# Sixteen heads of 8 on one core: the stack's ones by DMA, its zeros on VectorE, the first loads among the weights

## The reference

```python
x = x + L0_xattn(layernorm(x), ctx);  x = x + L0_ffn(layernorm(x))   # a0, f0
x = x + L1_xattn(layernorm(x), ctx);  x = x + L1_ffn(layernorm(x))   # a1, f1
x = x + L2_xattn(layernorm(x), ctx);  x = x + L2_ffn(layernorm(x))   # own, cross, f2
x = x + L3_xattn(layernorm(x), ctx);  x = x + L3_ffn(layernorm(x))   # a3, f3
```

```python
qh = heads(q @ Wq + bq);  kh = heads(k @ Wk + bk);  vh = heads(v @ Wv + bv)   # H = 16, D = 8
attn = softmax(einsum('bhqd,bhkd->bhqk', qh, kh) / sqrt(8), axis=-1)
out = concat(einsum('bhqk,bhkd->bhqd', attn, vh)) @ Wo + bo
```

## Time and profile before

| | |
|---|---|
| median of three runs | 8348.56 us |
| the profiled execution, its own time | 8347.76 us |
| its span | 8346.0 us |
| mean granted TensorE clock | 0.924 of full speed |
| busy: PE, VectorE, ACT, POOL | 7304.8, 5939.8, 4935.5, 2515.7 us |
| load blocks of a0, a1, a3 begin | 6.27, 1848.45, 6711.54 us |

### The profile page before, as it was taken

One profiled execution on the slowest core, in us unless ns is written; L12 is line 12 of the kernel. 1 busy time (PEld: TensorE's weight loads), 2 busy tenths in 40 slices (PEclk: granted clock), 3 DMA queues, 4 the chain that ended last, 5 costly groups with the idle time before them and its releaser, 6 DMA issues. The chain is left out here.

```text
span 8346.0 us, 186132 instructions
## 1 busy us (share of the span) xinstructions
PE 7304.8 (88%) x73814; PEld 3269.2 (39%) x73814; DVE 5939.8 (71%) x12851; ACT 4935.5 (59%) x9814; POOL 2515.7 (30%) x2443
## 2 busy tenths in 40 slices
PE   5999999877999997677679999999998759999979
PEld 2333333352333333344424444444444523333335
DVE  3888888646888896666646666666665438888855
ACT  3777777635888884333345555555554228888852
POOL 4222222123211210343334445445444232212200
PEclk9999999987999998677879999999999769999989
DMA  3334433204334420000100000000000133334310
GB/s 84 79 91 95 90 79 79 52 17 94 83 78 95 94 64 28 15 14 13 41 16 9 8 7 8 7 8 7 5 4 18 47 69 88 82 85 95 85 29 13
DMA packets 318099, 412.61 MB, mean 49 GB/s; under 512 B 56341, under 2 KB 237861, under 8 KB 317240
## 3 DMA queue, kind: packets, MB, share of 16 engines
q1 hardware_dynamic: 315704, 400.18, 20.7%
q10 hardware_dynamic: 1536, 0.53, 0.0%
HBM read 225.41 MB, written 174.66 MB: 48 GB/s over the span
## 5 line engine op out<-in xcount | busy, mean ns | idle before, releaser
L669 ACT ACTIVATE a_probs<-scores_ps 128x512 f32<-128x512 f32 (+2 forms) x5248 | 2819.4, 589 | 495.9 <-PE scores_ps L587 401.7
L728 DVE TENSOR_REDUCE a_unit_max<-bank 128x1 f32<-128x512 f32 x3072 | 2002.6, 682 | 197.0 <-PE bank L574 185.7
L604 PE MATMUL bank<-a_probs,a_v_sb 128*9 128x256 f32 (+1 forms) x20992 | 1619.4, 380 | 51.3 <-ACT a_out_sb L676 51.2
L587 PE MATMUL scores_ps<-a_stack 64*128 64x256 bf16 (+1 forms) x10496 | 1379.4, 274 | 13.5 <-ACT a_probs L669 9.5
L1268 ACT ACTIVATE cross_probs<-scores_ps 128x512 f32<-128x512 f32 (+1 forms) x1792 | 869.4, 570 | 777.9 <-PE scores_ps L1165 777.9
L1348 DVE TENSOR_REDUCE cross_unit_max<-bank 128x1 f32<-128x512 f32 x1536 | 1005.3, 686 | 326.0 <-PE bank L1151 322.4
L574 PE MATMUL bank<-a_stack 63*128 63x512 bf16 (+2 forms) x3413 | 1199.6, 375 | 6.4 <-DMA a_stack<-a_stack_dram 2.2
L1435 POOL TENSOR_TENSOR cross_added<-cross_probs 128x1024 f32<-128x1024 f32 x384 | 902.9, 2351 | 949.3 <-PE bank L1198 860.3
L728 DVE TENSOR_REDUCE a_unit_max<-scores_ps 128x1 f32<-128x512 f32 x1536 | 1047.8, 682 | 180.6 <-PE scores_ps L574 175.5
L797 POOL CAST a_parts<-a_qk 128x512 bf16<-128x512 f32 (+3 forms) x240 | 125.9, 525 | 1933.2 <-ACT a_qk L688 1841.1
L574 PE MATMUL scores_ps<-a_stack 63*128 63x512 bf16 (+2 forms) x1707 | 640.2, 375 | 36.2 <-DMA a_stack<-a_stack_dram 33.6
(11 more groups left out here) (417 smaller groups left out, 10423.7 us busy)
## 6 DMA issues: line engine op xcount, KB each, us to landing
a_stack_dram<-a_parts SPq DMA_DIRECT2D x288, 400.2 KB, 4.3
a_stack<-a_stack_dram SPq DMA_DIRECT2D x256, 348.2 KB, 7.9
a_stack<-a_stack_dram SPq DMA_DIRECT2D x128, 444.2 KB, 9.6
a_ctxT<-in_ctxT SPq DMA_DIRECT2D x48, 400.2 KB, 4.9
a_stack_dram<-a_parts SPq DMA_DIRECT2D x288, 64.0 KB, 2.6
a_stack_dram<-a_parts SPq DMA_DIRECT2D x96, 128.0 KB, 2.6
f_x<-x_after_dram SPq DMA_DIRECT2D x32, 256.0 KB, 3.2
x_after_dram<-a_res SPq DMA_DIRECT2D x48, 128.0 KB, 4.9
```

Source lines behind the costliest of these rows:

```text
L587: ins = pe.matmul(score_bank[(2 * e.i + a) % 3][0:n, j * TOK + q0:(j + 1) * TOK], stack[p][rows(a, 64), 2 * e.g + j, k0:k0 + n], stack[p][ ...
L604: ins = pe.matmul(out_bank[32 * h:32 * h + V8, q0:TOK], v[0:n, e.t, 4 * e.g + h, :], A.probs[0:n, held, o + q0:o + TOK], start=(e.t == 0), ...
L669: act.activation(by_pair(A.probs[0:n, b, a * 512:(a + 1) * 512])[:, :, q0:TOK], by_pair(score_bank[(2 * e.i + a) % 3][0:n, :])[:, :, q0:TO ...
L728: ins = dve.tensor_reduce(unit_max[:, e.g % 2, qt, 2 * a + j, c:c + 1], bank[:, 0:e.s.chunks[c][1]], AX.X, ALU.max)
```

## The change

- `prepare` no longer fills the stacks. It sets one tile `ones_k` of 16 partitions by KW columns to one (KW is 1857 or 1601), and in the values only the ninth column of each head.
- The zeros of both stacks are set by VectorE at the end of the bias block.
- The ones of rows 48 to 63 and 112 to 127 are copied from `ones_k` by four DMAs at the head of SP's part of the main block; each writes 16 partitions by 8 by KW. TensorE waits for them ahead of its first unit.
- ctxT and x of batch 0 are loaded in the load block, behind the weights.
- The five splits of the lead-in are made by VectorE and no longer by POOL; those of later batches stay on POOL.

```diff
@@ prepare
-            for s in stack:
-                chain(pool.memset(s[:, :, KW:W], 0.0))
-                for a in range(2):
-                    chain(pool.memset(s[64 * a + 32:64 * a + 64, :, 0:KW], 1.0))
+            chain(pool.memset(ones_k[:, :], 1.0))
             for vs in v_sb:
                 for v in vs:
-                    chain(pool.memset(v[:, :, :, :], 1.0))
+                    chain(pool.memset(v[:, :, :, 8:9], 1.0))
             L.prepare(pool, chain)
 
-        load_weights(nc, ctx, stage, [(W_sb[n][...], w[n]) for n in names_w + names_b], prepare)
+        load_weights(nc, ctx, stage, [(W_sb[n][...], w[n]) for n in names_w + names_b] + [
+            (ctxT[0][:, :], G.ctxT[0]), (x_sb[0][:, :, :], x_in[0].rearrange("(t p) c -> p t c", p=P))], prepare)
@@ bias block, VectorE
                 dve.memset(out_bank[:, :], 0.0)
+                for held in stack:
+                    dve.memset(held[:, :, KW:W], 0.0)
@@ new function
+        def split(eng, e):
+            made = e.cur + 1
+            c, k = piece(e.j), n_pieces * made + e.j + 1
+            eng.wait_ge(S["side_done"], e.after)
+            if e.j == 0 and made >= 1:
+                eng.wait_ge(S["parts_out"], 16 * outs * made)
+            eng.tensor_copy(parts[:, 0, c], qk[:, c]).then_inc(S["part0"], 1)
+            eng.wait_ge(S["part0"], k)
+            eng.tensor_tensor(qk[:, c], qk[:, c], parts[:, 0, c], ALU.subtract).then_inc(S["left"], 1)
+            eng.wait_ge(S["left"], k)
+            eng.tensor_copy(parts[:, 1, c], qk[:, c]).then_inc(S["part1"], 1)
+            eng.wait_ge(S["part1"], k)
+            eng.tensor_tensor(parts[:, 2, c], qk[:, c], parts[:, 1, c], ALU.subtract).then_inc(S["part2"], 1)
@@ program_sync
-            sp.dma_start(ctxT[0][:, :], G.ctxT[0]).then_inc(S["ctx_in"], 16)
-            sp.dma_start(x_sb[0][:, :, :], x_in[0].rearrange("(t p) c -> p t c", p=P)).then_inc(S["x_in"], 16)
+            for held in stack:
+                for a in range(2):
+                    sp.dma_start(held[64 * a + 48:64 * a + 64, :, 0:KW],
+                                 ones_k[:, :].rearrange("p (j n) -> p j n", j=1).to_broadcast([16, HEADS // 2, KW])
+                                 ).then_inc(S["ones_in"], 16)
@@ program_pe
                 if e.kind == "unit":
+                    if e.u == 0:
+                        pe.wait_ge(S["ones_in"], 64)
@@ program_dve
+                if e.kind == "split" and made == 0:
+                    split(dve, e)
@@ program_pool
-                if e.kind == "split":
...
+                if e.kind == "split" and made >= 1:
+                    split(pool, e)
```

More of the change, by code:

```diff
@@ L405, in attention8 @@
         v_sb = [[sb(f"v_sb{i}{p}", [P, s.T, HEADS, V8]) for i, s in enumerate(sources)] for p in range(2)]
+        ones_k = sb("ones_k", [16, KW], BF16)
         junk = sb("junk", [P, 2, TOK]) if with_self else None
@@ L424, in attention8 @@
         out_bank, side_bank = G.bank[0], G.bank[1]
-        S = Sems(nc, ctx, stage, ["x_in", "ctx_in", "ahead_in", "x_res_in", "ln_done", "side_ps", "side_done", "part0", "left",
+        S = Sems(nc, ctx, stage, ["ones_in", "ahead_in", "x_res_in", "ln_done", "side_ps", "side_done", "part0", "left",
                                   "part1", "part2", "parts_out", "stacked_first", "stacked_rest", "max_in0", "max_in1", "max_scores0", "max_scores1",
@@ L615, in program_pe @@
                     if e.kind == "k_cross":
-                        if made == 0:
-                            pe.wait_ge(S["ctx_in"], 16)
-                        else:
+                        if made >= 1:
                             pe.wait_ge(S["ahead_in"], 32 * made)
@@ L733, in program_dve @@
                                           negate=True).then_inc(S["max_rows"], 1)
+                if e.kind == "split" and made == 0:
+                    split(dve, e)
                 if e.kind == "ln_stats":
-                    if made == 0:
-                        dve.wait_ge(S["x_in"], 16)
-                    else:
+                    if made >= 1:
                         dve.wait_ge(S["ahead_in"], 32 * made)
```

## The result

| | before | with the change |
|---|---|---|
| median | 8347.03 us (8323.68 to 8351.48, 4 runs) | 8218.39 us (8211.68 to 8228.61, 4 runs) |
| ratio to before | | 0.9853, 95% interval 0.9831 to 0.9874 |
| the profiled execution, its own time | 8347.76 us | 8223.36 us |
| its span | 8346.0 us | 8221.6 us |

The change takes 1.5% off. 8218 us was forecast.

A forecast was written before the change was run, and what follows sets the result against it. POOL's memsets of ones were taken as the whole path at three stage starts. Load and bias blocks -131.4 us plus lead-ins +1.7 made -129.7 against 8347.8, so 8218 us; own range 8208 to 8245.

The forecast's parts named there:

- The load and bias blocks: From the last weight's issue to the first projection: 18.2, 12.5 and 13.3 us in a0, a1, a3, gaining 131.4 us.
- The zero memsets: VectorE's two memsets ending the bias block, uncovered: 3.9 us each in a0, 1.95 in a1 and a3, 15.6 in all.
- my lower bound of half: VectorE's zero memsets in the bias block might cost half of 15.6 us, as its cast to bf16 pays 0.50 ns per element.
- The lead-in: First projection to reading the stack: 8.8 us from faster splits eaten by the ones, +1.7 us over three starts.
- The walk of the splits: Lead-in splits on VectorE, stepped through from the first projection T: done by T + 12.2, writes starting 3 us sooner.
- The ones' rate: Four DMAs of ones ahead of the writes: 97 GB/s, geometric middle of 56 and 168; 19.6 us in a0, 16.9 elsewhere.
- The steady state: The time behind the three stage starts: left as it is, so each microsecond taken from a start comes off the whole.
- The clock: TensorE's clock in the lead-ins: gives and takes nothing, being at 0.50, the lower level, before a3 either way.
- Harmless ones: Lead-in copies run at 150 GB/s or more and early writes count: -140.2 us, 8208 us; chance 0.22.
- slow ones: Lead-in copies at 50 to 65 GB/s, writes queue behind them in every start: -90.5 us, 8257 us; chance 0.2.
- a single engine: One DMA engine carries the repeated-source copies of ones at 25 GB/s: +20.8 us, 8369 us, slower than before; chance 0.03.
- The Trainium skill's rule on ports: Bandwidth follows ports reached; partitions 48 to 63 reach four: ones at 84 GB/s, lead-ins +9.9 us, total 8226.

## Why the prediction was right, and where it was only lucky

**The load and bias blocks** came as worked out. From the last weight's issue to T I had 18.2, 12.5 and 13.3 us; measured are 18.8, 13.4 and 13.0. The gains are 45.9, 41.5 and 42.8, in all 130.2 us for the 131.4 forecast. SP ends the load block, as forecast, with the bias block at 18.47 for my 18.4.

**The zero memsets** were costed at 3.9 us in a0 from the recorded time of the one memset there was the earlier trace rows. The record says 3.47 us, but the next one starts 4.28 us after it: 0.8 us of gap are part of it. Two of them thus made a0's bias block 8.6 us longer (I had 7.8), those of a1 and a3 some 4.3 (3.9). The cost goes by the element, 1.04 ns each in bf16 and in float32, so my lower bound of half is out. This agrees with what the Trainium skill ("VectorE: DVE Perf Modes", section "Zero memsets can be issued as uint32 (trn2)") says of memsets, and so does the run with words, which took half. On POOL, behind SP's loads, the zeros cost nothing.

**The lead-in** is where the sum's term was mis-sized. I had +1.7 us from two parts, 8.8 gained by the faster splits and 10.5 lost to the ones; it was +7.0. Both parts were too small. The splits gain 13.7 us where nothing stands ahead of the writes, since the whole chain behind them, SP's issues and the last landing, moves up with them. The ones cost 22 us, by the run that takes half of them off the queue. Together that is +8.3, so the two runs agree with the +7.0 to 1.3 us. The parts aren't separate prices, though: with the ones ahead, the splits can go back to POOL at no loss.

The walk of the splits was right (first write at T + 11.1 for T + 12.2). The ones' rate came out at 101 GB/s for my 97, but that is luck: 97 was the middle of two bounds, and no row spoke for it. In a0 the ones are over at about T + 20, where I had T + 21. What was mis-sized is the stretch from there to the reading: I had 8.9 us for the writes at 407 GB/s and 1.5 for the landing, 10.4 in all, and it took 13.2. The 407 came from one microsecond in which the tall writes of the keys ran alone. In the run with the ones out of DRAM, where SP's issues are early and the DMA engines never idle, the same stretch takes 13.6 us: 379 GB/s from 52 to 58 us, but only 216 from 58 to 64, where the parts of the queries, in shorter rows, and the loads of batch 1 are under way. With the change SP is held as well (9.78 us over four copies, 12.90 over six writes) and comes to the parts of the queries only at T + 24; but without that hold the reading isn't sooner in a0. Which of the two, the slow last writes or SP's late issues, is the longer with the change isn't shown; SP still waits 0.9, 3.2 and 1.3 us for the parts to land. The stack was read at 33.1, 29.7 and 27.8 where I had 31.5, 26.9 and 26.9.

**The steady state** is untouched, as forecast: 7989.4 and 7989.1 us. That they agree so closely is chance, as the last section shows. The clock gave and took nothing either: the lead-in of a0 has a granted clock of 1.00 before and after, that of a3 0.50 before and after.

The sum -130.2 + 7.0 = -123.2 us, with -0.8 from the two stretches behind the reading and a rounding, is the measured -124.1 us of the starts; forecast were -129.7. That the median of the first four runs fell on 8218 is chance: the second four gave 8226, and the error in the starts was 5.6 us. (With the 0.8 us that I meant to add, my own sum makes 8219.)

**The rivals.** Harmless ones are refuted by the 22 us, slow ones by the 101 GB/s, and a single engine by the DMA share of 98%. The Trainium skill's rule on ports, for which I had set 84 GB/s and 8226 us, is the best account of the rate: the runs with 32 partitions and with DRAM as source agree with it, as far as they go. Its rate was too low and mine nearly right, yet its lead-ins (+9.9 us) are nearer to the +7.0 measured than mine (+1.7): I had the writes behind the ones too fast, and a slower rate of the ones made up for that.

## What to carry to other kernels

Ahead of a stage, look for the chain on which all engines wait at a barrier; POOL's memsets of a large tile cost by the elements of one partition (0.84 ns each here), and only a small part of them may be needed. When you hand such a fill to DMAs, give them a place on the queue behind whatever is urgent: a copy into 16 partitions holds all DMA engines at less than a third of the rate that the writes behind it reached (101 and 336 GB/s). Don't price a whole queue at the rate of its best microsecond. The ones on another engine's queue weren't tried. And put a new memset where another engine's wait covers it; at the end of a block every microsecond of it is paid.

## What the runs showed that I had not expected

- **SP is held at its issues, but not always.** Four copies of ones took 9.78 us to issue with the change, 6.64 with twice the partitions and 1.76 out of DRAM; two took 1.40. The six writes behind them took 12.90, 10.91, 2.81 and 4.39. The DMA engines were as busy with the copies out of DRAM as with the others, so their backlog alone doesn't explain it; what does is open.
- **A memset's record is shorter than its cost.** On VectorE 4096 elements are recorded as 3.47 us and take 4.28 from start to start; 2048 in bf16 as 1.76 and 2056 in float32 as 1.77, and both take 2.14.
- **A small DMA on ACT's queue waits too.** The row of maxima, 2 KB, arrived late while SP's copies of ones were in flight: 5.6 us from its issue to the first scores, and 2.8 with the copies behind it. With the 1.7 us ahead of it a0's first scores came 4.5 us sooner (25.0 to 20.5 us).
- **The rest of the span varies by itself.** Outside the three starts the profiled executions of all kernels range from 7964.5 to 8010.3 us, most of it in a0 and the stages from a1 to f2. In the second profile of the changed kernel a0 and f0 take 1724.3 us from the first scores to a1, in the first 1706.2, and the granted clock of the same stretch is 0.96 instead of 0.99. First profile:

```profile
474.00:874.00 400.00, 377.16 (x4100) 156.26 (x4093) 348.57 (x860) 313.61 (x640) 102.63 (x138) 0.99 0.41 94
```

Second profile of the same kernel:

```profile
474.00:874.00 400.00, 377.39 (x3984) 156.17 (x3981) 341.52 (x851) 306.57 (x624) 101.45 (x138) 0.96 0.37 86
```

TensorE is busy as long in both and gets fewer instructions done (3984 for 4100). What makes the clock differ was not tried. A gain of 5 us can't be read from one time of this kernel; in the timeline of the start it can.
